# A fused attention and mixture-of-experts layer on one core: the step loop written out, and linear attention by a per-group Q and V projection instead of a Gram matrix

## Chip, core and metric

One core of a Trainium2 chip runs the whole layer in one launch. The metric is the device time of that launch in microseconds (us). TensorE is called PE here, VectorE DVE, ScalarE ACT, GpSimd POOL; SP is the engine whose queue issues all transfers.

## What is computed

The input x is 8 sequences of 2048 rows of 256 floats. Two residual blocks follow each other, all in float32:

```python
x = x + attn(layernorm(x), wq, wk, wv, wo)
x = x + ffn(layernorm(x), Wr, router_bias, Wg, Wu, Wd, conv_w, conv_b)

def attn(x, wq, wk, wv, wo):        # per sequence, D = 64, no softmax
    Q = x @ wq.T;  K = x @ wk.T;  V = x @ wv.T
    energy = K.T @ V                # 64 x 64
    return (Q @ energy) * sqrt(3 / D) @ wo.T
```

The second block takes the top 2 of 8 sigmoid scores per row. Four experts are gated MLPs (256 to 128 to 256), the other four are the row itself or its relu; a causal depthwise convolution of 4 taps over the sequence is added. The launch sees 16384 rows; the attention's energy is per 2048 rows.

## The kernel before

**Groups and steps.** The 16384 rows are 32 groups of 512. A step works on several groups at once, each in another stage: L (first layernorm, `norm1_stats` and `norm1`) for group s, A (transposes of the normalised rows `xn`, and their Gram matrix) for s-1, B (attention, residual sum, second layernorm) for s-5, R (transposes of `x2`, router logits, top 2) for s-6, C (the four experts and the convolution) for s-7, Y (last down product, output) for s-8. The table `LAG` holds these distances. There are 40 steps. Each of the five engines has a `body(st)` that lists what it does in a step, in order; engines meet at semaphores alone. `steps` emits steps 0 to 7 as straight code, 8 to 31 as a hardware loop of four steps per iteration (`eng.Fori`, L295), and 32 to 39 as straight code again (SP leaves its loop one iteration earlier).

**Attention before.** It uses that K.T @ V is Wk (xn.T xn) Wv.T. Per group, `gram_matrix` (L435, L437) adds xn.T xn into a PSUM bank of its own, `ps_gram`. Every fourth step (`st.chain()`) a chain of small products turns the sum over four groups into a 256 x 256 matrix M: `chain_gramT`, `chain_p1`, `chain_et`, `chain_f`, `chain_m` on PE, each followed by a copy on ACT, and `m_hi`, `m_lo` at its end. `attention` then multiplies the transposed rows `xnT_hi`, `xnT_lo` by M: 24 matmuls of 256 columns per group, since a product of two split numbers is three matmuls (`three`, L371 to L373) and the 256 inputs are two chunks.

**Experts.** `gate_up(k)`, k = 0 to 7, are six matmuls of 512 columns each into three PSUM banks in turn; `down(e)` are twelve of 256. Between them, per expert e: `silu(e)` on ACT; `gate_weight(e)` on POOL (L1042), which multiplies by the routing weights `cwb`; `hidden(e)` on DVE (L786); `hid_high(e)` on ACT; `hid_low(e)` on DVE (e even) or POOL (e odd).

**Routing.** `router` on PE, the copy `logits` on ACT, a power on POOL (`enx`, L1059), `route` on DVE (L856 to L892), a transpose of the weights on PE (`weights_transpose`, L511), the copy `cwT` on ACT (L757 of the source, recorded at the helper's line L622). Then SP stores `cwT` to memory and loads it back broadcast over the partitions as `cwb`, which `gate_weight(0)` of the next step needs.

**One buffer that matters.** `x2` has two halves. `norm2` on ACT (L688) writes the half of group s-5, which is the half that C of the same step, group s-7, reads until DVE's sum of the relu term (L973) is done. So norm2 waits for the semaphore `relu_added` of the same step. This wait is in both kernels.

Of the kernel before, what the change touches and what calls it, by code (L numbers as in the profile page):

```python
# [25 lines left out]
F32 = mybir.dt.float32  # L26
# [13 lines left out]
class Step:  # L40


    def __init__(self, r, s, groups):
        self.r, self.s, self.groups = r, s, groups
        self.peeled = isinstance(r, int)

    def on(self, stage):

        return not self.peeled or 0 <= UNROLL * self.r + self.s - LAG[stage] < self.groups

    def was_on(self, stage):


        return not self.peeled or 0 <= UNROLL * self.r + self.s - 1 - LAG[stage] < self.groups

    def later(self, stage, n):

        return not self.peeled or UNROLL * self.r + self.s - LAG[stage] >= n
# [14 lines left out]
    def before(self, stage, per=1, extra=0):  # L73

        n = self.s - LAG[stage]
        if self.peeled:
            return per * min(max(UNROLL * self.r + n, 0), self.groups) + extra
        return self.r * (UNROLL * per) + (n * per + extra)
# [6 lines left out]
    def chains(self, per=1, extra=0):  # L85
# [3 lines left out]
        if self.peeled:  # L89
            return per * min(max(self.r + k, 0), self.groups // UNROLL) + extra  # L90
        return self.r * per + (k * per + extra)
# [9 lines left out]
def program(nc, x, wq, wkT, wvT, woT, wr, rbias, wg, wu, wd, convwb, cw_rows, out):  # L101
# [12 lines left out]
    LOOP = (LAG["Y"] // UNROLL, NG // UNROLL)  # L114
# [5 lines left out]
    with ctx:  # L120
# [12 lines left out]
        wvT_sb = sb("wvT_sb", [P, HC, D])  # L133
# [24 lines left out]
        xnT_hi = sb("xnT_hi", [P, 4, HC, GT], F32R)  # L158
        xnT_lo = sb("xnT_lo", [P, 4, HC, GT], F32R)

        gram = sb("gram", [P, 4, P])
        p1 = sb("p1", [P, HC, D])
        et = sb("et", [D, D])
        ff = sb("ff", [D, H])
        m_hi = sb("m_hi", [P, HC, H], F32R)
        m_lo = sb("m_lo", [P, HC, H], F32R)
# [42 lines left out]
        ps_gram = bank("ps_gram")  # L209
# [5 lines left out]
        w_loaded = sem("w_loaded")  # L215
        xa_loaded = [sem(f"xa_loaded{k}") for k in range(2)]
# [19 lines left out]
        gram_done = sem("gram_done")  # L236
        gram_out = sem("gram_out")
        gramT_done, gramT_out = sem("gramT_done"), sem("gramT_out")
        p1_done, p1_out = sem("p1_done"), sem("p1_out")
        et_done, et_out = sem("et_done"), sem("et_out")  # L240
        f_done, f_out = sem("f_done"), sem("f_out")
        m_done, mhi_out, mlo_out = sem("m_done"), sem("mhi_out"), sem("mlo_out")

        xnT_done = sem("xnT_done")
        xnThi_ready = sem("xnThi_ready")
        xnTlo_ready = sem("xnTlo_ready")
# [40 lines left out]
        N_LOADS = 7 + 2 * EM + 1  # L287
# [18 lines left out]
        def _(sp):  # L306
# [9 lines left out]
            sp.dma_start(wq_sb[:, :], wq).then_inc(w_loaded, 16)  # L316
            sp.dma_start(wkT_sb[:, :, :], wkT.rearrange("(c p) d -> p c d", p=P)).then_inc(w_loaded, 16)
            sp.dma_start(wvT_sb[:, :, :], wvT.rearrange("(c p) d -> p c d", p=P)).then_inc(w_loaded, 16)
# [9 lines left out]
            def body(st):  # L328
                if st.on("I") and not (st.peeled and st.group("I") < 2):
                    load_x(st)  # L330
# [7 lines left out]
                if st.on("R"):  # L338
# [8 lines left out]
                    if st.peeled and st.before("R") < 2:  # L347
# [13 lines left out]
            steps(sp, body, LOOP[1] - 1)  # L361
# [6 lines left out]
        def _(pe):  # L368
# [55 lines left out]
            def gram_matrix(st):  # L424

                pe.wait_ge(xn_ready, st.before("A", TG, TG))
                if st.first("A") and st.chain():
                    pe.wait_ge(mlo_out, st.chains(1, 1))  # L430
# [680 lines left out]
```

## Time and profile before

| | us |
|---|---|
| median of 3 runs | 1014.47 (1012.42 to 1015.83) |
| the profiled execution: its own time | 1023.05 |
| its span, first to last instruction | 1021.3 |
| PE busy | 944.8 (93%) |
| DVE busy | 807.6 (79%) |
| POOL busy | 560.1 (55%) |
| ACT busy | 506.2 (50%) |
| mean granted TensorE clock | 0.953 |

The median lies 8.6 us under the profiled execution's own time. Matmuls overlap each other in the records: a row's duration runs from the reading of its operands to its modelled end, so the cost of a matmul in a row of them is the distance between two starts. Many copies stand at one helper line (L622), so the rows are told apart by their tiles.

### The profile page before, as it was taken

How to read it: one execution, taken by the hardware profiler on the slowest of the kernel's cores; microseconds unless marked ns; L12 is line 12 of the kernel's file. 1: busy time of each engine (PE TensorE's matmuls, PEld its weight loads, DVE VectorE, ACT ScalarE, POOL GpSimd, SP SyncE). 2: the span in 40 equal slices, each digit the busy share in tenths (PEclk: the TensorE clock that was granted, in tenths of full speed). 3: DMA queues.
4: the chain of work that ended last, by engine and by line, in shares of the span. 5: the costliest groups of instructions: out<-in, count | busy, mean ns of one | idle time of the engine just before them, and what ended most of it. 6: DMA issues, size and time to landing. Idle time of an engine off the chain costs nothing.

```text
span 1021.3 us, 18818 instructions
## 1 busy us (share of the span) xinstructions
PE 944.8 (93%) x5816; PEld 828.5 (81%) x5816; DVE 807.6 (79%) x2294; ACT 506.2 (50%) x1003; POOL 560.1 (55%) x491
## 2 busy tenths in 40 slices
PE   4779999979999799997999979999899999988886
PEld 4568978968898688987888978988789898777775
DVE  6657878977689778996878968996888987777875
ACT  3455546544456454553555535555356554444342
POOL 2136656646566366664556655565566664565653
PEclk9779979998799899998999979999799999999999
DMA  5321222221222221223312222222022222122111
GB/s 175 104 76 51 80 86 104 104 84 51 73 103 103 83 76 48 103 103 104 103 62 83 79 86 103 103 97 89 21 103 103 83 83 83 63 83 83 63 49 56
DMA packets 60987, 86.64 MB, mean 85 GB/s; under 512 B 4480, under 2 KB 56832, under 8 KB 56832
## 3 DMA queue, kind: packets, MB, share of 16 engines
q1 hardware_dynamic: 60928, 86.01, 24.2%
q8 instruction: 17, 0.28, 0.1%
q14 instruction: 42, 0.34, 0.1%
HBM read 68.96 MB, written 17.04 MB: 84 GB/s over the span
## 4 chain that ended last, share of the span: by engine, by line
PE 58%; DVE 11%; issue 11%; POOL 10%; ACT 4%; DMA 3%; SPq 1%; POOLq 0%; DVEq 0%; ACTq 0%
PE ps_gu L371 8%; PE ps_gu L373 7%; PE ps_gu L372 7%; PE ps_sh L476 5%; POOL enx L1059 4%; PE ps_y L371 4%; PE ps_y L372 4%; PE ps_y L373 4%; PE ps_gram L435 3%; POOL gate L1042 3%; PE ps_y L419 2%; PE ps_sh L371 2%; PE ps_sh L372 2%; PE ps_sh L373 2%; POOL rstd L1024 2%
## 5 line engine op out<-in xcount | busy, mean ns | idle before, releaser
L1042 POOL TENSOR_TENSOR gate<-gate,cwb 128x512 f32<-128x512 f32 x128 | 176.6, 1380 | 207.4 <-ACT gate L629 127.8
L371 PE MATMUL ps_gu<-x2T_hi,wgu_hi 128*128 128x512 f32 x512 | 218.1, 426 | 2.3 <-DVE hid L786 2.3
L373 PE MATMUL ps_gu<-x2T_hi,wgu_lo 128*128 128x512 f32 x512 | 208.4, 407 | 0.0
L372 PE MATMUL ps_gu<-x2T_lo,wgu_hi 128*128 128x512 f32 x512 | 208.3, 407 | 0.0
L1059 POOL TENSOR_TENSOR enx<-inv_e,logits 128x32 f32<-128x32 f32 x32 | 184.8, 5773 | 42.2 <-ACT logits L622 42.1
L629 ACT ACTIVATE gate<-ps_gu 128x512 f32<-128x512 f32 x128 | 75.9, 593 | 178.5 <-PE ps_gu L373 178.5
L371 PE MATMUL ps_y<-wd_hi,hid_hi 128*128 128x256 f32 x512 | 153.3, 299 | 4.0 <-POOL hid_lo L1047 3.5
L803 DVE SCALAR_TENSOR_TENSOR conv<-x2T,conv_w,conv 128x512 f32<-128x512 f32 x192 | 147.0, 805 | 0.1
L372 PE MATMUL ps_y<-wd_lo,hid_hi 128*128 128x256 f32 x512 | 144.9, 283 | 0.0
L373 PE MATMUL ps_y<-wd_hi,hid_lo 128*128 128x256 f32 x512 | 144.8, 283 | 0.0
L371 PEld LDWEIGHTS ps_gu<-x2T_hi,wgu_hi 128*128 128x128 f32 x512 | 100.7, 197 | 24.3 <-DVE hid L786 6.3
L373 PEld LDWEIGHTS ps_gu<-x2T_hi,wgu_lo 128*128 128x128 f32 x512 | 100.2, 196 | 23.9
L786 DVE TENSOR_TENSOR hid<-ps_gu,gate 128x512 f32<-128x512 f32 x128 | 86.4, 675 | 33.9 <-PE ps_gu L373 26.4
L372 PEld LDWEIGHTS ps_gu<-x2T_lo,wgu_hi 128*128 128x128 f32 x512 | 100.7, 197 | 14.7
L1021 POOL TENSOR_TENSOR mv<-mv,eps_ln 128x4 f32<-128x4 f32 x64 | 12.7, 199 | 179.3 <-DVE mv L835 151.7
L1047 POOL TENSOR_TENSOR hid_lo<-hid,hid_hi 128x512 fp32r<-128x512 f32 x64 | 98.9, 1546 | 16.2 <-ACT hid_hi L622 16.2
L371 PEld LDWEIGHTS ps_y<-wd_hi,hid_hi 128*128 128x128 f32 x512 | 98.3, 192 | 6.8 <-POOL hid_lo L1047 4.6
L622 ACT ACTIVATE hid_hi<-hid 128x512 fp32r<-128x512 f32 x128 | 80.1, 626 | 47.7 <-DVE hid L786 45.2
L372 PEld LDWEIGHTS ps_y<-wd_lo,hid_hi 128*128 128x128 f32 x512 | 97.9, 191 | 1.4
L476 PEld LDWEIGHTS ps_sh<-wr_sb,x2T 128*128 128x128 f32 x512 | 69.8, 215 | 33.7 <-DVE x2T_lo L898 29.2
L373 PEld LDWEIGHTS ps_y<-wd_hi,hid_lo 128*128 128x128 f32 x512 | 96.9, 189 | 0.0
L476 PE MATMUL ps_sh<-wr_sb,x2T 128*128 128x8 f32 x512 | 69.3, 271 | 28.9 <-DVE x2T_lo L898 28.9
(94 smaller groups left out, 1974.5 us busy)
## 6 DMA issues: line engine op xcount, KB each, us to landing
cwb<-cw_rows SPq DMA_DIRECT2D x32, 1024.0 KB, 4.7
xa<-in_x SPq DMA_DIRECT2D x32, 512.0 KB, 6.5
acc<-in_x SPq DMA_DIRECT2D x32, 512.0 KB, 5.8
out<-acc SPq DMA_DIRECT2D x64, 256.0 KB, 2.2
cwb<-in_wg SPq DMA_DIRECT2D x4, 128.0 KB, 2.8
cwb<-in_wu SPq DMA_DIRECT2D x4, 128.0 KB, 2.8
cwb<-in_wd SPq DMA_DIRECT2D x1, 512.0 KB, 4.9
cw_rows<-cwT SPq DMA_DIRECT2D x32, 8.0 KB, 1.4
```

The source lines that it names most:

```text
L371: nc.tensor.matmul(dst, a_hi, b_hi, start=start, stop=False, skip_group_check=True)
L372: nc.tensor.matmul(dst, a_hi, b_lo, start=False, stop=False, skip_group_check=True)
L373: return nc.tensor.matmul(dst, a_lo, b_hi, start=False, stop=stop, skip_group_check=True)
L435: nc.tensor.matmul(ps_gram[:, 0:H], xn[:, q, t, 0:P], xn[:, q, t, :], start=start, stop=stop, skip_group_check=True)
L476: last = nc.tensor.matmul(b[:, t * NE:(t + 1) * NE], x2T[:, q, c, PAD + t * P:PAD + (t + 1) * P], wr_sb[:, c], start=(c == 0), stop=(c == ...
L622: return nc.scalar.activation(dst, src, ACT.Copy, scale=scale)
L629: nc.scalar.activation(gate[:, e % 2], ps_gu[GU_BANK[2 * e]][:, :], ACT.Silu)\
L786: v.tensor_tensor(hid[:, e % 2], ps_gu[GU_BANK[2 * e + 1]][:, :], gate[:, e % 2], ALU.mult)\
L803: v.scalar_tensor_tensor(conv[:, c], x2T[:, q, c, k:k + GT], conv_w[:, c, k:k + 1], conv[:, c], ALU.mult, ALU.add).then_inc(conv_ready, 1)
L1042: g.tensor_tensor(gate[:, e % 2], gate[:, e % 2], cwb[:, q, e], ALU.mult).then_inc(gatew_ready, 1)
L1047: g.tensor_tensor(hid_lo[:, 1], hid[:, 1], hid_hi[:, 1].bitcast(F32), ALU.subtract)\
L1059: g.tensor_tensor(enx[:, :], inv_e[:, :], logits[:, :], ALU.pow).then_inc(enx_ready, 1)
```

## The change

1. `steps` emits all 40 steps as straight code on every engine; there is no loop and no register arithmetic.
2. The Gram matrix, its bank and M are gone. Per group, PE transposes `xn` (as before), multiplies it by Wq and Wv side by side (`qv_project`, float32, two matmuls of 512 columns), transposes the result back (`qv_transpose`, 4), and multiplies `xn` by the rows of V (`p1_partial`, 8 float32 matmuls of 64 columns). ACT copies `xnT` (2), `qvT`, `q_hl` and `v_rows`; DVE makes the low half of Q (`q_low`) and adds up `p1` (`p1_add`).
3. The chain every fourth step has two products left, `chain_et` and `chain_f`, and `attention` has 8 matmuls of 256 columns with a 64-wide contraction stacked to 128.
4. The bank `ps_a` serves all these in turn, and the router.
5. Steps are reordered. On ACT the `logits` copy stands right behind silu(1), and norm2 before cwT, hid_high(3) and norm1. On DVE two of three tap pairs of the convolution come first, the residual sums stand between the experts' products, and `route` before hidden(2); p1_add and the sum of the relu term end the step.

```diff
-        def steps(eng, body, stop=LOOP[1]):
-            for r in range(LOOP[0]):
-                for s in range(UNROLL):
-                    body(Step(r, s, NG))
-            with eng.Fori(LOOP[0], stop, 1) as r:
-                for s in range(UNROLL):
-                    body(Step(r, s, NG))
-            for r in range(stop, ROUNDS):
+        def steps(body):
+            for r in range(ROUNDS):
                 for s in range(UNROLL):
                     body(Step(r, s, NG))
...
+            def qv_project(st):
+                pe.wait_ge(wqT_out, 1)
+                for c in range(HC):
+                    pe.wait_ge(xnT_ready, st.before("A", HC, HC if c or not early(st) else 1))
+                    if c == 0 and early(st) and st.later("A", 1):
+                        pe.wait_ge(p1_ready, st.before("A"))
+                    last = nc.tensor.matmul(ps_a[:, :], wqv[:, c], xnT[:, c], start=(c == 0), stop=(c == HC - 1))
+                last.then_inc(qv_done, 1)
+            def qv_transpose(st):
+                pe.wait_ge(qvT_ready, st.before("A", 1, 1))
+                for t in range(TG):
+                    last = nc.tensor.transpose(ps_a[:, t * P:(t + 1) * P], qvT[:, t * P:(t + 1) * P], ident[:, :])
+                last.then_inc(vrows_done, 1)
+            def p1_partial(st):
+                pe.wait_ge(vrows_ready, st.before("A", 1, 1))
+                q = st.slot("A", 2)
+                for c in range(HC):
+                    for t in range(TG):
+                        last = nc.tensor.matmul(ps_a[:, c * D:(c + 1) * D], xn[:, q, t, c * P:(c + 1) * P],
+                                                v_rows[:, t], start=(t == 0), stop=(t == TG - 1))
+                last.then_inc(p1_done, 1)
...
                 for k in range(2):
                     tok = slice((2 * h + k) * P, (2 * h + k + 1) * P)
-                    for c in range(HC):
-                        last = three(b[:, k * H:(k + 1) * H], xnT_hi[:, q, c, tok], xnT_lo[:, q, c, tok],
-                                     m_hi[:, c], m_lo[:, c], c == 0, c == HC - 1)
+                    at = slice(k * H, (k + 1) * H)
+                    nc.tensor.matmul(b[:, at], q_hl[:, q, tok], ff_hi[:, :], start=True, stop=False,
+                                     skip_group_check=True)
+                    last = nc.tensor.matmul(b[:, at], q_hl[:, q, tok], ff_lo[:, :], start=False, stop=True,
+                                            skip_group_check=True)
...
@@ PE body, the new order of a step's second half
+                if a_on:
+                    xn_transpose(st, 0)
+                if b_on:
+                    attention(st, 0)
                 if c_on:
                     gate_up(st, 4)
+                if a_on:
+                    xn_transpose(st, 1)
                 if c_on:
                     conv_transpose(st)
                     down(st, "C", 0)
+                if b_on:
+                    attention(st, 1)
                 if c_on:
+                    gate_up(st, 5)
+                if a_on:
+                    qv_project(st)
+                if c_on:
                     gate_up(st, 6)
                     down(st, "C", 1)
+                if a_on:
+                    qv_transpose(st)
+                if c_on:
                     gate_up(st, 7)
                 if a_on:
+                    p1_partial(st)
                 if r_on:
                     weights_transpose(st)
                 if c_on:
                     down(st, "C", 2)
```

Where the end of a step moved on DVE. Before, in the middle of a step (the first `hid` row is hidden(1), the `acc<-x,coef,acc` rows add the identity experts, `acc<-acc,x` is the sum of the relu term):

```order
L792 TENSOR_TENSOR hid_lo<-hid,hid_hi 128x512 [waits hidhi_ready]
L786 TENSOR_TENSOR hid<-ps_gu,gate 128x512 [waits hidlo_ready1,gu_done,gatew_ready]
L963 SCALAR_TENSOR_TENSOR acc<-x,coef,acc 128x256 [waits rt]
L963 SCALAR_TENSOR_TENSOR acc<-x,coef,acc 128x256 x3
L973 TENSOR_TENSOR acc<-acc,x 128x1024 [waits relu_ready]
L786 TENSOR_TENSOR hid<-ps_gu,gate 128x512 [waits hidlo_ready0,gu_done,gatew_ready]
L856 TENSOR_SCALAR den<-enx 128x32 [waits enx_ready]
```

Now, from the end of `route` on (hidden(2), hid_low(2), q_low, hidden(3), p1_add, the sum of the relu term, then the next step):

```order
L902 TENSOR_TENSOR coef<-cw 128x4 [waits cw_ready]
L796 TENSOR_TENSOR hid<-ps_gu,gate 128x512 [waits hidlo_ready0,gu_done,gatew_ready]
L802 TENSOR_TENSOR hid_lo<-hid,hid_hi 128x512 [waits hidhi_ready]
L918 TENSOR_TENSOR q_hl<-qvT,q_hl 64x512 [waits qhi_ready]
L796 TENSOR_TENSOR hid<-ps_gu,gate 128x512 [waits hidlo_ready1,gu_done,gatew_ready]
L931 TENSOR_TENSOR p<-ps_a,p 128x128 [waits p1_ready,p1_done]
L1022 TENSOR_TENSOR acc<-acc,x 128x1024 [waits relu_ready]
L970 COPY x2T<-x2T 128x2x3 [waits conv_ready,x2T_ready]
```

The sum of the relu term moved from before hidden(2) to the very end of the step, behind the addition of `p1`.

The end of a step on ACT before, in the loop (norm1, cwT, the high parts of `xnT`, hid_high(3) between them, norm2 last):

```order
L677 ACTIVATE xn<-xa,shift,rstd 128x256 [waits xnT_done,gram_done,shift1_ready]
L677 ACTIVATE xn<-xa,shift,rstd 128x256 x3
L756 REGISTER_ALU [waits cwT_done]
L622 ACTIVATE cwT<-ps_sh 16x128 [waits cw_stored]
L666 REGISTER_ALU
L622 ACTIVATE xnT_hi<-ps_sh 128x512 [waits xnT_done]
L622 ACTIVATE hid_hi<-hid 128x512 [waits down_done,hid_ready]
```

```order
L688 ACTIVATE x<-acc,shift,rstd 128x256 [waits x2T_done,relu_added,shift2_ready]
L688 ACTIVATE x<-acc,shift,rstd 128x256 x3
L295 REGISTER_ALU
L295 COMPARE_AND_BRANCH
L629 ACTIVATE gate<-ps_gu 128x512 [waits hid_ready,gu_done]
```

And now:

```order
L609 ACTIVATE hid_hi<-hid 128x512 [waits down_done,hid_ready]
L609 ACTIVATE v_rows<-ps_a 128x256 [waits p1_done,vrows_done]
L701 ACTIVATE x<-acc,shift,rstd 128x256 [waits x2T_done,relu_added,shift2_ready]
L701 ACTIVATE x<-acc,shift,rstd 128x256 x3
L609 ACTIVATE cwT<-ps_sh 16x128 [waits cw_stored,cwT_done]
L609 ACTIVATE hid_hi<-hid 128x512 [waits down_done,hid_ready]
L690 ACTIVATE xn<-xa,shift,rstd 128x256 [waits p1_done,shift1_ready]
```

norm2, with its wait for `relu_added`, moved ahead of cwT, hid_high(3) and norm1; the copy `v_rows` stands behind hid_high(2).

## Rows read from the trace of the kernel before

**Rows 1.** The page's first part: busy time of each engine.

```profile
PE 944.8 (93%) x5816; PEld 828.5 (81%) x5816; DVE 807.6 (79%) x2294; ACT 506.2 (50%) x1003; POOL 560.1 (55%) x491
```

**Rows 2.** Stretches: us; busy and count of PE, PEld, DVE, ACT, POOL; clock; DMA.

```profile
69.80:854.90 785.10, 756.75 (x4707) 669.05 (x4705) 646.61 (x1842) 408.57 (x814) 450.08 (x384) 0.95 0.24 86
705.70:743.10 37.40, 31.54 (x179) 27.82 (x178) 25.89 (x72) 15.89 (x31) 19.29 (x16) 0.86 0.21 71
717.20:727.50 10.30, 9.00 (x30) 7.74 (x31) 9.12 (x21) 0.83 (x3) 5.11 (x1) 0.50 0.15 51
743.10:773.80 30.70, 30.70 (x200) 26.45 (x198) 25.53 (x72) 16.95 (x37) 17.80 (x18) 1.00 0.23 86
773.80:800.60 26.80, 26.80 (x178) 24.36 (x177) 23.38 (x71) 14.83 (x29) 15.83 (x13) 1.00 0.28 98
854.90:1021.30 166.40, 143.78 (x879) 120.75 (x876) 119.87 (x313) 70.65 (x140) 89.61 (x60) 1.00 0.21 74
```

**Rows 3.** The waits: who waited for whom, us in total, times, longest.

```profile
PE ps_sh L476 <- DVE x2T_lo L898: 28.9, 7, 5.8
```

**Rows 4.** Timeline of DVE behind the loop's branch: start, us, instruction [idle before].

```profile
713.60 1.17 DVE L938 COPY x2T<-x2T 128x6 f32<-128x6 f32 x1 [6.04 <-issue]
```

**Rows 5.** Timeline of PE in one chain step, 504 to 529 us.

```profile
504.01 1.10 PE L525 MATMUL ps_gram<-wvT_sb,gram 128*128 128x64 f32 x8
...
518.74 0.28 PE L371 MATMUL ps_sh<-m_hi,xnT_hi 128*128 128x256 f32 x1
...
521.61 0.40 PE L371 MATMUL ps_gu<-x2T_hi,wgu_hi 128*128 128x512 f32 x1
...
525.84 0.59 PE L435 MATMUL ps_gram<-xn 128*128 128x256 f32 x2
...
528.57 0.60 PE L451 MATMUL ps_sh<-ident,xn 128*128 128x128 f32 x4
```

**Rows 6.** Timeline of ACT, two ends of steps.

```profile
741.15 0.27 ACT L622 ACTIVATE cwT<-ps_sh 16x128 f32<-16x128 f32 x1 [2.56 <-PE ps_sh L511]
...
794.06 2.07 ACT L677 ACTIVATE xn<-xa,shift,rstd 128x256 f32<-128x256 f32 x4
```

**Rows 7.** Timeline of POOL: routing weights' arrival, the power, one gate product.

```profile
747.85 1.28 POOL L1042 TENSOR_TENSOR gate<-gate,cwb 128x512 f32<-128x512 f32 x1 [2.91 <-DMA cwb<-cw_rows]
...
793.73 1.30 POOL L1042 TENSOR_TENSOR gate<-gate,cwb 128x512 f32<-128x512 f32 x1 [0.58 <-ACT gate L629]
...
809.63 5.43 POOL L1059 TENSOR_TENSOR enx<-inv_e,logits 128x32 f32<-128x32 f32 x1
```

**Rows 8.** Timeline of DVE in a regular step, 783 to 801 us.

```profile
783.04 1.40 DVE L803 SCALAR_TENSOR_TENSOR conv<-x2T,conv_w,conv 128x512 f32<-128x512 f32 x2
784.37 0.68 DVE L792 TENSOR_TENSOR hid_lo<-hid,hid_hi 128x512 fp32r<-128x512 f32 x1
...
785.57 1.66 DVE L963 SCALAR_TENSOR_TENSOR acc<-x,coef,acc 128x256 f32<-128x256 f32 x4
787.83 1.23 DVE L973 TENSOR_TENSOR acc<-acc,x 128x1024 f32<-128x1024 f32 x1 [0.59 <-ACT x L733]
...
791.01 0.49 DVE L856 TENSOR_SCALAR den<-enx 128x32 f32<-128x32 f32 x1
...
793.87 1.20 DVE L875 TENSOR_TENSOR chosen<-hot 128x32 f32<-128x32 f32 x1
795.10 0.19 DVE L877 TENSOR_TENSOR raw<-chosen,score 128x32 f32<-128x32 f32 x1
...
796.30 0.68 DVE L792 TENSOR_TENSOR hid_lo<-hid,hid_hi 128x512 fp32r<-128x512 f32 x1
796.91 1.28 DVE L824 TENSOR_TENSOR acc<-ps_sh,acc 128x512 f32<-128x512 f32 x2
798.22 1.40 DVE L832 BATCH_NORM_STATS2 stats<-acc 128x6 f32<-128x256 f32 x4
...
800.02 0.65 DVE L786 TENSOR_TENSOR hid<-ps_gu,gate 128x512 f32<-128x512 f32 x1
```

More of the change, by code:

```diff
@@ L328, in body @@
             def body(st):
-                if st.on("I") and not (st.peeled and st.group("I") < 2):
+                if st.on("I") and st.group("I") >= 2:
                     load_x(st)
@@ L441, in xn_transpose, with early @@
-            def xn_transpose(st, c):
-                pe.wait_ge(xn_ready, st.before("A", TG, TG))
-                if c == 1 and st.on("R"):
-                    pe.wait_ge(cwT_ready, st.before("R", 1, 1))
-                elif st.on("B"):
-                    pe.wait_ge(x1_ready, st.before("B", 2, 2 - c))
-                elif st.later("A", 1):
-                    pe.wait_ge(xnTlo_ready, st.before("A", HC, c - 1))
-                for t in range(TG):
-                    last = nc.tensor.transpose(ps_sh[c][:, t * P:(t + 1) * P],
+            def early(st):
+                return not st.on("R") and not st.on("B")
@@ L899, in x2T_low, with f_low, q_low, p1_add @@
                     .then_inc(x2Tlo_ready, 1)
+            def f_low(st):
+                dve.wait_ge(fhi_out, st.chains(1, 1))
+                v.tensor_tensor(ff_lo[:, :], ps_a[:, 0:H], ff_hi[:, :].bitcast(F32), ALU.subtract).then_inc(flo_out, 1)
+            def q_low(st):
+                k = st.slot("A", 4)
+                dve.wait_ge(qhi_ready, st.before("A", 1, 1))
+                v.tensor_tensor(q_hl[D:P, k], qvT[0:D, :], q_hl[0:D, k].bitcast(F32), ALU.subtract)\
+                    .then_inc(qlo_ready, 1)
+            def p1_add(st):
+                dve.wait_ge(p1_done, st.before("A", 1, 1))
+                now = ps_a[:, 0:HC * D].rearrange("p (c d) -> p c d", c=HC)
+                if st.first("A"):
+                    if st.later("A", 1):
+                        dve.wait_ge(et_done, st.chains())
+                    v.tensor_copy(p1[:, :, :], now).then_inc(p1_ready, 1)
+                else:
+                    dve.wait_ge(p1_ready, st.before("A"))
+                    v.tensor_tensor(p1[:, :, :], now, p1[:, :, :], ALU.add).then_inc(p1_ready, 1)
             def split_weights():
@@ L955, in body @@
                     conv_tap(st, 2)
+                if st.on("L") and c_on:
+                    norm1_stats(st)
+                if c_on:
                     hid_low(st, 0)
+                if b_on:
+                    residual(st, 0)
+                if c_on:
                     hidden(st, 1)
@@ L964, in body @@
                             .then_inc(ident_added, 1)
-                if m_on:
-                    dve.wait_ge(mhi_out, st.chains(1, 1))
-                    v.tensor_tensor(m_lo[:, :, :], ps_gram[:, :].rearrange("p (c n) -> p c n", c=HC),
-                                    m_hi[:, :, :].bitcast(F32), ALU.subtract).then_inc(mlo_out, 1)
+                if b_on:
+                    residual(st, 1)
+                    norm2_stats(st)
+                if r_on:
+                    route(st)
+                if c_on:
+                    hidden(st, 2)
+                    hid_low(st, 2)
+                if st.on("A"):
+                    q_low(st)
+                if c_on:
+                    hidden(st, 3)
+                if st.on("A"):
+                    p1_add(st)
                 if c_on:
```

309 lines of the change are left out of this document (137 added, 172 removed).

## The prediction

> **What bounds the kernel now.** I read the page's busy shares first: PE is busy 93% of the span, DVE 79% [rows 1]. Then the stretches, each cut where a step's first gate/up matmul starts. A regular step takes 26.8 us and PE is busy in all of it; DVE works 23.4 us of it [rows 2] (the stretch from 773.8). So in a regular step PE's own work is the bound, and nothing ends a wait on it. A step with the chain takes 30.7 us, PE busy throughout [rows 2] (from 743.1). A third kind takes 37.4 us [rows 2] (from 705.7): it is the first step of a loop iteration. There DVE sits idle for 6.04 us with nothing to wait for (released by "issue") behind the loop's branch [rows 4], its x2T_lo comes late, and PE's router waits for that, 5.8 us at most and 28.9 us in all [rows 3]. Right behind, the granted clock stands at 0.50, TensorE's 1.2 GHz level, for 10.3 us [rows 2] (from 717.2); before, PE had stood idle. Such a step loses 37.4 - 26.8 = 10.6 us. The first 26 of the 32 steps with experts take 785.1 us together; the last six and the end take 166.4 us [rows 2].
>
> **The change part by part.**
>
> *The loop's branch.* Five iterations end inside the 26 steps; with straight code the branch and its idle time are gone, up to 5 x 10.6 = 53 us. The Trainium skill's page Runtime: NRT & Kernel Launch (Instruction fetch mechanics) says that a taken branch breaks the sequential prefetch while straight code streams; the trace agrees, since the straight stretches show no such row.
>
> *PE's work in a regular step.* Attention: 24 matmuls from 518.74 to 521.61, 2.87 us, 0.12 each [rows 5]; now 8, 0.96. Gram: 525.84 to 528.57 less one small transpose of 0.11, 2.62 us for 1536 float32 columns, 1.7 ns a column [rows 5]; gone. New: qv_project has 1024 float32 columns, 1.75 us by the same rate. Four transposes more take 0.35 (the block of four [rows 5] less the tail of 0.2 that runs beside the next matmul). p1_partial: 8 float32 matmuls of 64 columns, each recorded as two, 16 records; 8 such took 1.10 us with their tail [rows 5], so about 1.8. Changes of operand type cost some 0.2. Sum: -1.91 - 2.62 + 1.75 + 0.35 + 1.8 + 0.2 = -0.4, so PE needs 26.4 us. In the chain step three of five products go, at most 3.9 us less (30.7 - 26.8).
>
> If PE stayed the bound, the 26 steps would now take about 26 x 26.4 + 6 x 0.8 = 691 us. I don't believe that it does, because of a ring of waits that closes in each step.
>
> *The ring.* I follow it from the first matmul of p1_partial to the same one a step later.
> 1. p1_partial 2.0 us with its tail [rows 5]; then DVE's p1_add, a read of PSUM of 128 columns that no row shows. Between 0.2 (a small DVE operation [rows 8] (L877)) and 0.7 (512 columns [rows 8] (L792)); 0.3, nearer the small one.
> 2. DVE's sum of the relu term, now behind p1_add: 1.23 [rows 8] (L973).
> 3. ACT's norm2 waits for it: four activations, 2.0 by the same four of norm1 [rows 6]; then cwT 0.27 [rows 6].
> 4. The store, the load of the broadcast weights and their landing: from the end of cwT at 741.42 to POOL's gate product at 747.85, 6.4 us [rows 6, 7]. Before, cwT ended well ahead of the step's end; now all of this lies on the ring.
> 5. gate_weight(0) 1.3 [rows 7].
> 6. DVE, start to start: hidden(0) 0.6, the third tap pair 1.33, norm1_stats 1.8 (as norm2_stats from 798.22 to 800.02), hid_low(0) 0.6, residual(0) 0.65, hidden(1) 0.6, the identity sums 1.66, residual(1) 0.65, norm2_stats 1.8: 9.7 us [rows 8].
> 7. route, 791.01 to 796.30: 5.3 [rows 8].
> 8. hidden(2) 0.65, hid_high(2) 0.5 and v_rows 0.4 on ACT with their hand-overs (by the pitch of ACT's rows [rows 6]): 1.6. Then PE may start p1_partial.
>
> Sum: 2.3 + 1.25 + 2.3 + 6.4 + 1.3 + 9.7 + 5.3 + 1.6 = 30.15 us. That is more than PE's 26.4, so PE would idle nearly 4 us per step: before p1_partial above all, and before down(3) of the next step, whose low half now comes late, since hid_high(3) stands behind norm2.
>
> *Collisions.* A small DVE sum took 1.20 us instead of 0.19 while POOL ran a gate product from 793.73 to 795.03 [rows 7, 8]: the two engines exclude each other there. On the ring the third tap pair starts while gate_weight(1) runs, which follows gate_weight(0) at once: +0.6. And two gate products and enx (1.3 + 1.3 + 5.43 = 8.0 us [rows 7]) end about when the identity sums start (1.3 + 0.6 + 0.6 + 1.33 + 1.8 + 0.6 + 0.65 + 0.6 = 7.5 us from the same start [rows 8]), so gate_weight(2) falls among them: +1.3, once a gate product's length. Lower bound 0, upper bound two POOL products, 2.6. That gives 30.15 + 1.9 = 32.05; I take 32.0. The Trainium skill (SBUF — State Buffer, Who interferes with whom) calls this an exclusive lock that the first comer keeps for the whole instruction; were each identity sum first, DVE would lose nothing there and POOL would wait, and the ring would be 30.7.
>
> The bounds of the ring: 29.3 (weights landing 0.5 sooner, no collision, route without POOL's product, some 0.4 to 1 less) to 34.5 (both collisions doubled, and half clock now and then).
>
> *Chain steps.* et is covered by the wait for down(3). The copies on ACT and f_low stand before hidden(0): 0.8 us per chain, six times: 5 us.
>
> *Sum against the profiled execution.* 26 x 32.0 + 5 = 837, less 3 for the first (no output) and last (no norm1_stats): 834 against 785.1, +49. Behind them group stage A is over, and the ring closes without p1_partial at about 27.5, as long as the 27.7 of now (166.4 / 6): -3. Ahead of the first expert step A's hand-overs are longer, route comes sooner: -1. Together +45: the span goes from 1021.3 to 1066. On the median, which lies 8.6 us under the profiled run's own time of 1023.05, that is 1014.5 + 45 = **1060 us**.
>
> **The rivals.**
>
> *The ring at its lower end* (29.3 to 30.2, middle 29.7): 26 x 29.7 + 2 = 774, -11, tail and start -4: 1000 us. Speaks for it: every collision is a guess about phase. Against: route took 5.3 with POOL beside it, and POOL's gate_weight(3) will stand there again. It decides at 30.2, where the 26 steps take what they take now.
>
> *PE stays near its own work; faster.* If the ring does not close through norm2, because p1_partial starts early enough that the relu sum is done before PE wants x2, only the wait for v_rows is left: route and hidden(2) end after gate_up(7), some 1.4 us. Then a step is 27.8, the 26 steps 727, -58, with the tail 955 us. For it: PE, DVE and ACT each have less than 27 us of work. Against: the order of rows shows the wait for `relu_added` right behind v_rows, and norm2 ahead of cwT. It decides where cwT ends 2 us before a step's end, as now. The Trainium skill's page on fetching says that kernels prefer full unrolling; by that alone this case would win.
>
> *The clock falls in most steps.* Now it fell behind PE's wait of 5.8 us [rows 2, 3]. The ring leaves PE idle for 2 to 3 us ahead of p1_partial's small matmuls. At half clock for up to 10.3 us [rows 2] PE loses up to 5.2 us; its idle time takes up some 3, so +2 per step, 26 x 2 = 52: 1112 us. Against: the last six steps have PE idle for 22.6 us in all at a clock of 1.00 [rows 2].
>
> *The straight code stalls too*, since five engines must fetch thousands of rows. The loop's loss of 53 us would come back only in part, as the ring already holds PE back: 1075 us.
>
> A change within 0.3% is about what a measurement of this kernel can tell from none.
>
> **How the numbers follow.** The ring near 32: 0.60. The lower end: 0.10, four fifths of it faster. PE-bound: 0.08. The clock: 0.17. Stalls: 0.05. The predicted time is that of the first, 1060. Its own range is 1035 to 1090 (31 to 33.2 us per step). The range for 8 in 10 takes in part of the lower end and the clock case: 1003 to 1113. Faster by over 0.3%: 0.08 + 0.06 = 0.14; within 0.3%: 0.04; slower: 0.82.
>
> **What would show it.** The five idle stretches of DVE released by "issue" are gone. Regular steps are 31 to 33 us apart, PE is busy under 90%, and PE waits for ACT's v_rows (2 us or more a step, about 25 times) and for POOL's hid_lo. ACT's norm2 waits for DVE's relu sum, POOL's first gate product for the DMA of cwb, in each step. Wrong would be: regular steps under 30 us; PE's main wait on something else than v_rows; norm2 not waiting for the relu sum.

## The result and the profile after

The changed kernel takes 1039.86 us (median of 4 runs, 1033.45 to 1041.67), the kernel before 1015.04 us in the same session (4 runs, 1012.42 to 1015.83). The ratio is 1.0238, with a 95% interval of 1.0189 to 1.0286: slower by 2.4%. The profiled execution of the changed kernel took 1041.67 us, with a span of 1039.9 us, so all sums below are made against spans: 1039.9 - 1021.3 = +18.6 us. Between the medians it is 24.8 us; the profiled execution of the kernel before took 1023.05 us, 8.0 more than the median of 1015.04.

The busy shares of the changed kernel, in the columns of [rows 1]:

```profile
PE 930.6 (89%) x5458; PEld 784.8 (75%) x5458; DVE 772.9 (74%) x2284; ACT 540.4 (52%) x1086; POOL 539.5 (52%) x491
```

PE has 14.2 us less to do than before, in a span that is 18.6 us longer. The stretches, in the columns of [rows 2]; each is again cut at the first gate/up matmul of a step:

```profile
10.75:85.37 74.62, 57.09 (x240) 39.88 (x240) 29.29 (x112) 37.29 (x71) 17.87 (x33) 0.74 0.21 66
85.37:876.90 791.53, 734.13 (x4421) 626.05 (x4420) 616.92 (x1843) 429.77 (x872) 435.75 (x385) 0.96 0.25 85
482.80:511.27 28.47, 26.88 (x170) 23.21 (x170) 22.31 (x70) 15.44 (x32) 17.02 (x15) 0.99 0.28 94
511.27:542.42 31.15, 28.36 (x178) 23.45 (x177) 24.30 (x73) 16.70 (x36) 16.38 (x15) 1.00 0.25 86
664.50:696.70 32.20, 29.31 (x172) 25.28 (x171) 24.67 (x75) 17.54 (x36) 16.99 (x15) 0.92 0.24 82
876.90:1039.90 163.00, 138.88 (x801) 118.57 (x799) 122.87 (x312) 69.66 (x137) 83.33 (x58) 0.95 0.22 75
```

The first gate/up matmul comes at 85.4 us instead of 69.8: +15.6. The 26 steps take 791.5 us instead of 785.1: +6.4. The last six steps and the end take 163.0 instead of 166.4: -3.4. Together these are the +18.6. The third to fifth lines are a regular step, a step with the chain, and a regular step of which a part runs at half clock. The waits, as in [rows 3]:

```profile
POOL hid_lo L1073 <- ACT hid_hi L609: 229.7, 32, 8.5
POOL gate L1068 <- DMA cwb<-cw_rows: 131.8, 29, 10.1
ACT x L701 <- issue: 100.2, 26, 4.7
PE ps_a L471 <- ACT v_rows L609: 45.9, 32, 2.0
PE ps_y L362 <- POOL hid_lo L1073: 16.3, 19, 1.8
```

PE waits in each step ahead of p1_partial (L471) for v_rows, for 1.55 to 2.0 us, and in 19 steps ahead of down(3) for POOL's hid_lo, which waits for hid_high(3) on ACT, which stands behind norm2 (L701). The profile puts norm2's own wait of up to 4.7 us down to "issue"; the timeline tells more. It shows one turn of the ring, from one p1_partial to the next, with ACT's, DVE's and POOL's rows put together in the order of the ring (start, us, instruction, idle before):

```profile
478.19 2.00 PE L471 MATMUL ps_a<-v_rows,xn 128*128 128x64 f32 x16 [1.55 <-ACT v_rows L609]
```

```profile
480.23 0.29 DVE L931 TENSOR_TENSOR p<-ps_a,p 128x128 f32<-128x128 f32 x1 [0.20 <-PE ps_a L471]
480.44 1.21 DVE L1022 TENSOR_TENSOR acc<-acc,x 128x1024 f32<-128x1024 f32 x1
```

```profile
481.74 2.08 ACT L701 ACTIVATE x<-acc,shift,rstd 128x256 f32<-128x256 f32 x4 [3.60 <-issue]
483.72 0.25 ACT L609 ACTIVATE cwT<-ps_sh 16x128 f32<-16x128 f32 x1
```

```profile
490.21 2.52 POOL L1068 TENSOR_TENSOR gate<-gate,cwb 128x512 f32<-128x512 f32 x2 [4.34 <-DMA cwb<-cw_rows]
492.70 5.87 POOL L1085 TENSOR_TENSOR enx<-inv_e,logits 128x32 f32<-128x32 f32 x1
498.54 1.70 POOL L1068 TENSOR_TENSOR gate<-gate,cwb 128x512 f32<-128x512 f32 x1
```

```profile
491.51 0.69 DVE L796 TENSOR_TENSOR hid<-ps_gu,gate 128x512 f32<-128x512 f32 x1 [1.10 <-POOL gate L1068]
492.12 1.82 DVE L813 SCALAR_TENSOR_TENSOR conv<-x2T,conv_w,conv 128x512 f32<-128x512 f32 x2
493.87 1.40 DVE L823 BATCH_NORM_STATS2 stats<-xa 128x6 f32<-128x256 f32 x4
...
497.43 1.65 DVE L1002 SCALAR_TENSOR_TENSOR acc<-x,coef,acc 128x256 f32<-128x256 f32 x4
...
501.51 0.14 DVE L866 TENSOR_SCALAR den<-enx 128x32 f32<-128x32 f32 x1
...
504.69 0.92 DVE L891 TENSOR_SCALAR wsum_eps<-wsum 128x4 f32<-128x4 f32 x1
...
506.21 0.69 DVE L796 TENSOR_TENSOR hid<-ps_gu,gate 128x512 f32<-128x512 f32 x1
```

```profile
506.93 0.63 ACT L609 ACTIVATE hid_hi<-hid 128x512 fp32r<-128x512 f32 x1 [2.25 <-DVE hid L796]
507.47 0.37 ACT L609 ACTIVATE v_rows<-ps_a 128x256 f32<-128x256 f32 x1
```

Norm2 starts 0.09 us after the relu sum ends (480.44 + 1.21 = 481.65), although the trace names no releaser. From 478.19 the next p1_partial starts at 507.89: 29.7 us. Between hidden(2) and p1_add two ways run side by side: v_rows and p1_partial, and on DVE itself hid_low(2), q_low and hidden(3). The second is only 0.20 us shorter: that is all that p1_add waits for PE (the row at 480.23). Nine of the regular turns measure 29.6 to 29.8 us, and three of the six with a chain 31.2.

### The profile page after: what moved, and what is told of

Its sections match the earlier page's. It is cut to its first block and busy times, and to the rows that moved or that the text cites. A ratio compares the mean times of both kernels' runs of the same rounds, so it can differ in the third digit from the quotient of the medians.

```text
span 1039.9 us, 16308 instructions
## 1 busy us (share of the span) xinstructions
PE 930.6 (89%) x5458; PEld 784.8 (75%) x5458; DVE 772.9 (74%) x2284; ACT 540.4 (52%) x1086; POOL 539.5 (52%) x491
## 5 line engine op out<-in xcount | busy, mean ns | idle before, releaser
L362 PE MATMUL ps_gu<-x2T_hi,wgu_hi 128*128 128x512 f32 x512 | 225.1, 440 | 0.0
L1073 POOL TENSOR_TENSOR hid_lo<-hid,hid_hi 128x512 fp32r<-128x512 f32 x64 | 82.3, 1286 | 229.7 <-ACT hid_hi L609 229.7
L362 PE MATMUL ps_y<-wd_hi,hid_hi 128*128 128x256 f32 x512 | 162.3, 317 | 27.7 <-POOL hid_lo L1073 16.3
L364 PE MATMUL ps_y<-wd_hi,hid_lo 128*128 128x256 f32 x512 | 152.3, 297 | 0.0
L363 PE MATMUL ps_y<-wd_lo,hid_hi 128*128 128x256 f32 x512 | 152.2, 297 | 0.0
L908 DVE TENSOR_TENSOR x2T_lo<-ps_sh,x2T_hi 128x512 fp32r<-128x512 f32 x64 | 44.0, 688 | 112.0 <-ACT x2T_hi L609 112.0
L701 ACT ACTIVATE x<-acc,shift,rstd 128x256 f32<-128x256 f32 x128 | 66.5, 591 | 111.0 <-issue 100.2
L471 PE MATMUL ps_a<-v_rows,xn 128*128 128x64 f32 x512 | 72.9, 302 | 45.9 <-ACT v_rows L609 45.9
L471 PEld LDWEIGHTS ps_a<-v_rows,xn 128*128 128x128 f32 x512 | 67.8, 213 | 58.7 <-ACT v_rows L609 58.7
L363 PEld LDWEIGHTS ps_y<-wd_lo,hid_hi 128*128 128x128 f32 x512 | 105.4, 206 | 1.3
```

The costliest lines, as they stand in the source:

```text
L362: nc.tensor.matmul(dst, a_hi, b_hi, start=start, stop=False, skip_group_check=True)
L363: nc.tensor.matmul(dst, a_hi, b_lo, start=False, stop=False, skip_group_check=True)
L364: return nc.tensor.matmul(dst, a_lo, b_hi, start=False, stop=stop, skip_group_check=True)
L471: last = nc.tensor.matmul(ps_a[:, c * D:(c + 1) * D], xn[:, q, t, c * P:(c + 1) * P], v_rows[:, t], start=(t == 0), stop=(t == TG - 1))
L701: nc.scalar.activation(x2[:, q, t], acc[:, st.slot("B", 4), t], ACT.Identity, bias=shift2[:, t:t + 1], scale=rstd2[:, t:t + 1]).then_inc(x ...
L1073: g.tensor_tensor(hid_lo[:, 1], hid[:, 1], hid_hi[:, 1].bitcast(F32), ALU.subtract)\
```

## The experiments

The theory was the ring of the prediction, only shorter than thought. The main rivals were the wait for v_rows alone, and the clock. All ratios below are to the kernel before on the same chip in the same session; the experiments ran in three further sessions, with medians of 1017.6, 1015.8 and 1017.6 us for the kernel before, so differences between kernels of two sessions carry 2 or 3 us of doubt.

### Straight code alone

The kernel before, with its loop written out:

```diff
-            for r in range(LOOP[0]):
-                ...
-            with eng.Fori(LOOP[0], stop, 1) as r:
-                ...
-            for r in range(stop, ROUNDS):
+            for r in range(ROUNDS):
                 for s in range(UNROLL):
                     body(Step(r, s, NG))
```

> The kernel before with its 40 steps written out and nothing else changed. Theory: the loop's branch costs what the profile of before shows at five iterations, 10.6 us each (DVE idle for about 6 us, then half clock), so the time falls by 45 to 53 us, to 962 to 970 us, and no DVE row is left with idle time released by issue of over 1 us. Rival: straight code has stalls of its own, since each engine must fetch every row once: then less than half of that comes back, over 990 us.

Measured: 972.8 us (970.95 to 977.41), ratio 0.956 (0.950 to 0.961), 44.8 us under the 1017.6 of the kernel before: close to the theory, though just outside its 962 to 970, and far from the rival's 990. Its 26 steps take 736.8 us, 48.3 less than the 785.1 of [rows 2]; that is 9.7 us for each of five branches, where the prediction had 10.6. The kernel before had DVE idle for 5.3 to 6.0 us ahead of the first row behind each of the five branches:

```profile
DVE x2T L938 <- issue: 17.1, 3, 6.0
DVE x2T L938 <- ACT x2T L622: 10.5, 2, 5.3
```

The straight code has no such row. The Trainium skill's page Runtime: NRT & Kernel Launch (Instruction fetch mechanics) names a taken branch as what breaks the sequential prefetch, and that agrees with these rows. So the rest of the change, the new attention and the new order together, costs some 67 us (1039.9 - 972.8). No run has one of the two without the other.

### The ring: relu sum early, v_rows first, and both

```diff
                 if c_on:
                     hidden(st, 2)
+                    dve.wait_ge(relu_ready, st.before("C", TG, TG))
+                    k = st.slot("C", 4)
+                    v.tensor_tensor(acc[:, k], acc[:, k], x2[:, st.slot("C", 2)], ALU.add)...
                     hid_low(st, 2)
```

(and gone from behind p1_add.)

> The changed kernel with DVE's sum of the relu term between hidden(2) and hid_low(2) instead of at the end of the step. Theory (the ring p1_partial, p1_add, relu sum, norm2, cwT, cwb, gate, hidden(0), route, hidden(2), v_rows sets the step): norm2 starts about 4 us sooner, the ring is cut, the wait of PE for v_rows of 1.6 us per step stays, steps go from 28.9 to 31 us down to about 28 to 29, the whole to 985 to 1005 us. Rival (only the wait for v_rows and the clock that falls behind it make the step longer): norm2's place is worth nothing, 1030 to 1042 us.

Measured: 998.6 us (992.62 to 1007.06), ratio 0.980 (0.973 to 0.986), as the theory had it.

```diff
-                if c_on:
-                    hid_high(st, 2)
                 if st.on("A"):
                     v_rows_out(st)
+                if c_on:
+                    hid_high(st, 2)
```

> The changed kernel with ACT's copy v_rows ahead of hid_high(2). Theory of the ring: PE's wait for v_rows is gone (1.6 us x 26), but DVE's relu sum still stands behind hidden(2), hid_low(2) and hidden(3), so the ring is only some 0.6 us shorter; PE's idle time moves to down(3), and the clock falls more rarely; 1000 to 1020 us. Rival (the wait for v_rows alone): all 1.6 us per step and the falls of the clock come back, under 985 us.

Measured: 1037.75 us (1036.48 to 1042.64), ratio 1.022 (1.015 to 1.028). That is the time of the changed kernel: a miss for the expectation. The wait for v_rows is gone from all but the first steps, and PE now waits in each step at another place, down(3):

```profile
ACT x L701 <- DVE acc L1022: 103.2, 30, 3.6
PE ps_y L362 <- POOL hid_lo L1073: 48.4, 32, 1.8
```

Here the profile names the releaser of norm2: DVE's relu sum. Where the changed kernel had 16.3 us on the second line, this one has 48.4. Its 26 steps take 790.1 us, as long as before, but for a reason that the expectation lacked. A regular turn, from one relu sum to the next, is now 30.5 us and not 29.7. From hidden(2) to the relu sum it is 0.3 us shorter (3.63 instead of 3.92), since DVE's own way was nearly as long as the one by v_rows. The rest of the turn grew by 1.1: from hidden(0) to route 10.60 us instead of 10.00, with a wait of 0.41 for the attention on PE, and route 5.07 instead of 4.70, as its small operation wsum_eps fell wholly beside gate_weight(3):

```profile
487.85 0.69 DVE L834 TENSOR_TENSOR acc<-ps_sh,acc 128x512 f32<-128x512 f32 x1 [0.41 <-PE ps_sh L513]
493.55 1.29 DVE L891 TENSOR_SCALAR wsum_eps<-wsum 128x4 f32<-128x4 f32 x1
```

So the ring sets the length of a step here too; v_rows was on it, but with a second way of almost its length beside it.

> Both edits: the relu sum between hidden(2) and hid_low(2), and v_rows ahead of hid_high(2). Theory: neither the ring nor the wait for v_rows is left, PE is the bound again with 26.4 to 26.8 us in a regular step and idle under 0.5 us, no fall of the clock in regular steps; the whole 945 to 965 us. Rival: another wait takes the place (hid_low(3) behind norm2, for down(3)): over 975 us.

Measured: 958.57 us (951.02 to 960.11), ratio 0.940 (0.933 to 0.946). Alone, the first move gives 41 us and the second nothing; together they give 81. The relu sum has not left the way to the weights: norm2 still starts 0.09 us behind it (415.63 + 1.22 = 416.85), although the profile names another engine:

```profile
415.63 1.22 DVE L1013 TENSOR_TENSOR acc<-acc,x 128x1024 f32<-128x1024 f32 x1
416.94 2.08 ACT L701 ACTIVATE x<-acc,shift,rstd 128x256 f32<-128x256 f32 x4 [0.56 <-POOL shift L1050]
```

It starts 0.61 us behind the start of hidden(2) where it was 3.92, so both ways to p1_add, 3.3 us, are what left the ring; that puts the ring at about 26.4 us, an estimate (29.7 - 3.3). This is how limits look that lie close to each other: the ring (29.7 us a step); then PE's work with its wait for v_rows, which stands on ACT behind hid_high(2) and so behind DVE's route and hidden(2) (28.05 us); and PE's own work under both. A regular step of the kernel with both:

```profile
385.00:412.00 27.00, 26.48 (x171) 23.00 (x170) 24.35 (x69) 16.69 (x34) 18.25 (x15) 1.00 0.30 99
```

PE's work is 26.48 us; the prediction had summed 26.4. The remaining 0.5 is a wait for hid_lo ahead of down(2).

### Norm2 behind the weights' copy, and all three moves

```diff
-                if st.on("B"):
-                    norm2(st)
                 if r_on:
                     ...
                     copy(cwT[:, :], ps_sh[1][0:EM * TG, 0:P]).then_inc(cwT_ready, 1)
                 if c_on:
                     hid_high(st, 3)
+                if st.on("B"):
+                    norm2(st)
```

> The changed kernel with ACT's norm2 moved behind the copy cwT and hid_high(3); nothing else. Theory A (the ring goes relu sum, norm2, cwT, store and load of the weights): the relu sum (1.2 us) and norm2 (2.0 us) leave the way to the weights, the ring falls from about 30 to 27 us, and what is left is the wait for v_rows of 1.5 us: regular steps of 27.5 to 28.5 us, 965 to 995 us in all. hid_high(3) comes 2 us earlier, so PE's wait for hid_lo ahead of down(3) goes as well. Rival B (the relu sum on DVE is what costs, by holding DVE and norm2 alike): 1030 to 1045 us, no change, and x2_transpose of the next step waits for x2 instead.

Measured: 1007.27 us (1002.07 to 1011.8), ratio 0.992 (0.988 to 0.995). The direction is that of theory A and rival B is out, but the gain is 33 us where 45 to 75 were expected. Undisturbed steps take the 28.05 us of the theory, and PE's wait for POOL's hid_lo is gone from the 26 steps; two things come on top. The wait ahead of p1_partial stays and half clock comes with it, and the chain steps take 30.5 to 33.7 us; in five of the six the router waits 0.84 to 0.87 us for f_low.

> The changed kernel with the three moves together: relu sum behind hidden(2), v_rows ahead of hid_high(2), norm2 behind hid_high(3). Theory A (with the first two moves the ring is already shorter than PE's own 26.5 us of work, so a third cut of it buys only the 0.5 us that PE still idles before the down products): 945 to 958 us, regular steps 26.6 to 27.0 us. Rival B (norm2 behind hid_high(3) comes too late for the next step's x2_transpose, which then waits): 965 to 985 us.

Measured: 977.69 us (975.42 to 983.25), ratio 0.964 (0.960 to 0.968). Rival B was right: the third cut costs 19 us against the kernel with two. Regular steps keep 27.05 us. In the six chain steps norm2's lateness passes through x2_transpose and f_low to the router, and right behind that wait the clock falls:

```profile
374.68 1.48 PE L495 MATMUL ps_a<-wr_sb,x2T 128*128 128x8 f32 x12 [1.10 <-DVE ff_lo L913]
```

```profile
376.90:380.30 3.40, 3.40 (x14) 2.81 (x12) 2.19 (x10) 0.85 (x2) 3.39 (x1) 0.50 0.00 0
```

### The new order in the old loop

The middle rounds of the changed kernel are put back into the hardware loop of the kernel before, with its register arithmetic; the order of the work stays.

> The changed kernel's order of work, with the middle rounds put back into the hardware loop of the kernel before. Only the form of the code differs. Theory A (five branches stall DVE for some 6 us each, a half clock follows, and the ring's own idle time on PE takes up only part of it, since the stalled engine lies on the ring): 5 x 6 to 5 x 9 us more than the changed kernel, 1068 to 1085 us. Rival B (the ring's slack takes up the stall, straight code is worth nothing here): 1036 to 1048 us.

Measured: 1060.34 us (1056.28 to 1065.88), ratio 1.042 (1.038 to 1.046), 20.5 us over the changed kernel. It lies between the two expectations. Its 26 steps take 818.5 us, 27 more than 791.5, so a branch costs 5.4 us here and 9.7 in the kernel before. DVE's idle time behind the branch is itself shorter:

```profile
DVE x2T L982 <- issue: 8.6, 5, 1.8
```

That is 1.7 us a branch instead of 5.3 to 6.0. So the smaller cost doesn't show that PE's idle time in the ring took up a stall of the old length, as both expectations had supposed; why the stall is shorter here was not taken apart.

### The start

The two moves of above, and f_low ahead of split_weights and norm1_stats in the steps before the first expert step:

```diff
+                if m_on and not c_on:
+                    f_low(st)
                 if st.group("L") == LAG["B"]:
                     split_weights()
...
-                if m_on:
+                if m_on and c_on:
                     f_low(st)
```

> Relu sum behind hidden(2) and v_rows ahead of hid_high(2), as in the kernel that had both, and in the steps ahead of the first expert step DVE does f_low before split_weights and norm1_stats. Theory A (the late start is a chain of hand-overs, and f_low behind split_weights holds the first attention): the first gate/up matmul comes 2 to 3 us earlier than the 85.3 of the kernel with both, the total is 955 to 957 us. Rival B (stage A's group by group chain sets the start and takes the gain back): first gate/up matmul at 84.5 to 86, the total within 1 us of 958.6.

Measured: 957.48 us (956.44 to 961.03), ratio 0.943 (0.939 to 0.947). The first gate/up matmul comes at 81.8 us instead of 85.3, but the medians of the two kernels can't be told apart. It isn't shown that f_low made all of the 3.5 us either: the same code ahead of the first expert step put that matmul at 78.5 to 88.3 us in other kernels, according to where the half clock fell. So the next kernel fills PE's waits in the first steps:

```diff
+            def fill(dst, n):
+                for _ in range(n):
+                    nc.tensor.transpose(dst[:, 0:P], ident[:, :], ident[:, :])
...
                 last.then_inc(qv_done, 1)
+                if not st.on("C"):
+                    fill(ps_y[0], 5)
```

(and in the same way behind xn_transpose, qv_transpose and p1_partial.)

> The kernel with the relu sum early, v_rows first and f_low first, and in the steps before the first expert step PE fills its short waits with 15 transposes of the identity into an unused bank (4 behind xn_transpose, 5 behind qv_project, 3 behind qv_transpose, 3 behind p1_partial); they add nothing to the result. Theory A (a stage A group costs about 7.6 us at the full granted clock and 10.2 at half clock, and the clock falls because PE waits often there): the granted clock of the stretch ahead of the first gate/up matmul stays near 1.0, the p1_partial blocks are 7.5 to 8.5 us apart, the first gate/up matmul comes at 73 to 77 us instead of 81.8, the total is 947 to 953 us. Rival B (the groups' distance is hand-overs alone, whatever the clock): first gate/up matmul at 82 to 90 us, the total 957 to 966 us.

Measured: 955.74 us (952.88 to 958.47), ratio 0.939 (0.934 to 0.944). The changed kernel's first groups, on PE's timeline:

```profile
22.86 3.56 PE L455 MATMUL ps_a<-xnT,wqv 128*128 128x512 f32 x4
27.11 0.66 PE L462 MATMUL ps_a<-ident,qvT 128*128 128x128 f32 x4 [0.69 <-ACT qvT L609]
28.25 2.56 PE L471 MATMUL ps_a<-v_rows,xn 128*128 128x64 f32 x16 [0.47 <-ACT v_rows L609]
31.28 1.94 PE L444 MATMUL ps_sh<-ident,xn 128*128 128x128 f32 x8 [0.47 <-DVE p L931]
...
38.48 2.55 PE L471 MATMUL ps_a<-v_rows,xn 128*128 128x64 f32 x16 [0.47 <-ACT v_rows L609]
```

and the filled kernel's p1_partial blocks, with its stretch up to the fall of the clock at 60.3:

```profile
18.27 2.00 PE L477 MATMUL ps_a<-v_rows,xn 128*128 128x64 f32 x16
25.87 2.00 PE L477 MATMUL ps_a<-v_rows,xn 128*128 128x64 f32 x16
33.48 2.00 PE L477 MATMUL ps_a<-v_rows,xn 128*128 128x64 f32 x16
```

```profile
16.00:60.30 44.30, 36.59 (x239) 27.15 (x238) 20.43 (x71) 26.05 (x50) 8.27 (x20) 1.00 0.22 73
```

A group takes 7.6 us at the full clock, and 10.2 in the changed kernel, where it runs in part at half clock. But a group without filling can take 7.6 us too. These rows are of the kernel of the next experiment, whose first steps are not filled:

```profile
24.71 2.00 PE L471 MATMUL ps_a<-v_rows,xn 128*128 128x64 f32 x16 [0.47 <-ACT v_rows L617]
32.32 2.00 PE L471 MATMUL ps_a<-v_rows,xn 128*128 128x64 f32 x16 [0.47 <-ACT v_rows L617]
```

There the clock first fell at 38.0 us; in the nine kernels without filling that share this stage it did so between 19 and 38 us, in the filled one not before 60.3. So it is shown what the clock costs a group, and filling goes with a later fall in the one trace that there is. The rest of theory A was missed: the next blocks were 9.1 and 11.5 us apart, at 60.3 us the clock fell for 10.2 us after all, and the first gate/up matmul came at 78.2, not at 73 to 77. That is no sooner than the 78.5 of the earliest kernels without filling, and the total can't be told from the 957.5 of the unfilled kernel.

### The wait ahead of p1_partial, filled

The kernel with only the relu sum early, and

```diff
+                if a_on and b_on and c_on:
+                    pe.wait_ge(x1_ready, st.before("B", 2, 1))
+                    fill(ps_sh[1], 10)
                 if a_on:
                     p1_partial(st)
```

> The kernel with only the relu sum early (998.6 us; PE idle for 1.55 us ahead of p1_partial in each step), and PE does 10 transposes of the identity in that wait, about 1.4 us; they add nothing to the result. Theory A (the idle time itself is not filled by work that counts, but it is what lets the clock fall; without it the half clock stretches go): steps without the chain 28.0 to 28.2 us apart nearly all of them, 26 steps in 735 to 745 us instead of 756.7, the total 975 to 987 us. Rival B (the clock falls for another reason, such as the small float32 matmuls behind the wait): 26 steps in 752 to 760 us, the total 994 to 1004 us.

Measured: 982.41 us (979.51 to 985.86), ratio 0.965 (0.960 to 0.969), 16 us under the same kernel without the ten transposes. The 26 steps of the one and of the other:

```profile
88.30:845.00 756.70, 717.14 (x4420) 615.58 (x4419) 655.88 (x1846) 437.04 (x878) 472.36 (x386) 0.97 0.26 89
```

```profile
78.45:825.74 747.29, 733.63 (x4682) 634.51 (x4681) 658.35 (x1846) 436.58 (x879) 472.71 (x386) 0.99 0.26 91
```

Behind the first, 19 of the 20 steps without a chain now take 28.0 to 28.3 us; before, they took up to 29.25. The 26 steps fall by 9.4 us, at 747.3 just short of the expected 735 to 745; the chain steps stay at 29.7 to 31.3. The two profiled executions lie 21.2 us apart by their spans (the medians 16.2): 9.4 in these steps, 9.8 at the start, whose code is the same in both (first gate/up matmul at 88.3 and 78.5), and 1.9 behind them. So 9 us or so is what the transposes are shown to give, and the difference at the start is luck. Useless work on PE made the steps shorter, through the clock: the undisturbed steps keep their 28.05 us, so v_rows came no sooner.

## Why the prediction was right and where it was off

The sign and the range held (slower; 1003 to 1113 us, and the narrower 1035 to 1090 of the first case). The forecast of 1060 was 20 us too high, and that hides two larger misses of opposite sign: -43 us in the 26 steps, +17 at the start. That the total fell within the narrower range is luck: its steps of 31 to 33.2 us did not come. Even the sign owes much to the start, which holds 15.6 of the 18.6 us by which the span grew. With the start as predicted the span would be 1023.3 us, 2 us over that of before (and some 8 over its median). What the mechanism gave is that the ring took back, and a little more, what the straight code had gained: +6.4 us in the 26 steps.

**The loop's branch.** Predicted up to -53 us, measured 26 steps shorter by 48.3 in the kernel before. Right in kind: no idle time of DVE by "issue" is left. The prediction priced all five branches by the longest of the five steps, 37.4 us; they measure 35.4 to 37.4. And the trace of before puts only three of the five idle stretches down to "issue", the other two to a copy on ACT.

**PE's work.** Predicted 26.4 us a step, measured 26.48.

**The ring.** It is there, link by link, in the order that the prediction gave; moving the relu sum ahead of what stood between it and hidden(2) takes 41 us. What the prediction didn't have is the second way beside v_rows and p1_partial, on DVE, 0.2 us shorter: because of it, taking away the wait for v_rows alone shortens that part by only 0.3 us, and other terms took that back. Its length was predicted as 32.0 us and measured as 29.7. By its terms, from the turn shown above (predicted, measured):

```
p1_partial and p1_add                2.3     2.25   478.19 to 480.44
relu sum                             1.25    1.30   to 481.74
norm2 and cwT                        2.3     2.23   to 483.97
store, load and landing of weights   6.4     6.24   to 490.21
first gate product                   1.3     1.30   to 491.51
DVE from hidden(0) to route         11.6    10.00   to 501.51
route                                5.3     4.70   to 506.21
hidden(2) to p1_partial              1.6     1.68   to 507.89
```

The term that was mis-sized is the two collisions, 1.9 us in all. The third tap pair took 1.82 us where 1.40 had been read [rows 8], +0.4 for the predicted 0.6. The identity sums took 1.65, as undisturbed as the 1.66 of [rows 8], for the predicted +1.3: POOL's power ran until 498.57, within the four sums, and the gate product behind it took 1.70 instead of 1.28. The wait fell to POOL, the outcome for which the prediction, in the sentence on the Trainium skill's page SBUF — State Buffer (Who interferes with whom), gave 30.7 us. Route was the second term: 4.7 us instead of 5.3. As in [rows 8], gate_weight(3) met one small operation of it, but cost it less (wsum_eps, 0.92 instead of 0.17, against 1.20 instead of 0.19), and its first operation took 0.14 us where 0.49 had been read [rows 8] beside another POOL product. That rival, the ring at its lower end, "29.3 to 30.2, middle 29.7", had been given a chance of 0.10; for the ring it was exact, but its total of 1000 us was not.

**Chain steps.** Predicted +0.8 us each, measured +1.5 for the ring (31.2 to 29.7): +4 us over six.

**The clock.** Neither the forecast nor the rival with half clock in most steps describes it. It fell in about half of the steps, mostly for 3.4 us. The 26 steps come to 791.5 us, and 26 x 29.7 + 6 x 1.5 to 781, so about 10 us are left for half clock and the first steps; the rival had 52.

**The start.** Predicted -1 us, measured +15.6. This term was not worked out from rows, only named ("hand-overs are longer, route comes sooner"). The rows above show it: four groups of stage A go through PE one after the other, each with transposes, a copy, qv_project, a copy, transposes, a copy, p1_partial and p1_add. In the changed kernel they start 10.2 us apart. In the kernel before, PE's timeline shows their transposes 5.4 us apart on average:

```profile
10.30 1.94 PE L451 MATMUL ps_sh<-ident,xn 128*128 128x128 f32 x8 [10.30 <-ACT xn L677]
...
15.66 1.04 PE L451 MATMUL ps_sh<-ident,xn 128*128 128x128 f32 x8
...
22.03 1.10 PE L451 MATMUL ps_sh<-ident,xn 128*128 128x128 f32 x8 [2.72 <-ACT xn L677]
...
26.43 1.09 PE L451 MATMUL ps_sh<-ident,xn 128*128 128x128 f32 x8 [0.68 <-ACT xn L677]
```

Of the 4.8 us more per group 2.2 are the longer way (7.6 at the full clock) and 2.6 the half clock on it; over four groups that is 19 us. What gave back the other 4 wasn't taken apart. The half clock part is not fixed: with the same code ahead of the first expert step, that step began at 78.5 to 88.3 us in the kernels above.

**The tail.** Predicted -3 us, measured -3.4.

**PE stays near its own work.** That rival named the wait for v_rows as 1.4 us and the step as 27.8; once the ring is cut by the relu sum, wait and step are 1.55 and 28.05. It was the next limit, not the first.

Of the rows that were to show each step, "Regular steps are 31 to 33 us apart" was wrong (28.1 to 32.3), and by the text's own measure "regular steps under 30 us" speaks against the size of the ring, though not against the ring. PE busy under 90% (89%), the waits for v_rows and hid_lo, and the first gate product's wait for cwb are as foretold; the wait for v_rows was 1.55 to 2.0 us, not 2 or more. The chance of "faster" is also mis-added: 0.08 for the lower end and 0.08 for the PE-bound rival make 0.16, not 0.14.

What stays open is why the clock fell in some steps of the changed kernel and not in others with the same wait of 1.55 us, how much of the 3.5 us at the start was f_low, and what the new attention is worth apart from the new order.

## What to carry to other kernels

When a step's engines all have less work than the step is long, write down the ring of waits from one instruction to itself a step later. Look at each link for a second way beside it: removing PE's wait for v_rows gave nothing, since a way on DVE was only 0.2 us shorter and other terms of the ring grew. Moving one addition of 1.2 us on DVE up by 3.3 us, past both ways, gave 41 us, until the next limit, and both together 81. A term that is only named, such as the start here, needs its rows as well: count the hand-overs of the first groups, when nothing else covers them.

## What was not expected of the hardware

Short waits of PE cost more than their length. With 1.55 us idle per step, the granted clock fell to 0.50 (the 1.2 GHz level) in many steps, for 3.4 us mostly. With ten transposes of no use in that wait, 19 of 20 regular steps were within 0.3 us of each other, and the 26 steps were 9.4 us shorter. At the start the first groups stood 7.6 us apart at the full clock, filled or not, and 10.2 apart where the clock had fallen; which of the two an unfilled kernel got differed from kernel to kernel.

POOL's power over 128x32 elements took 5.87 us beside DVE's sums of 128x256, and cost them nothing; POOL's 128x512 product that started within the same sums took 1.70 us instead of 1.28. A DVE operation of 0.17 us (wsum_eps) took 0.92 to 1.31 beside another such product.

The fastest kernels of the study are the one with both moves (958.6 us), with f_low first (957.5), and with the filled start (955.7). They can't be told from each other, and all are some 6% faster than the kernel before. Straight code alone gave 4.4% (972.8).
